# Rotated keys from exchanged half-head tiles, a mask by quarters, and a shorter correlation tail

## The reference

```python
x = x + tanh(g_xattn[0]) * attention_16_heads_of_8(norm(x), ctx, ctx)   # |i - j| > 64 masked
x = x + tanh(g_ffn[0])   * experts_8_top_2(norm(x))
x = x + tanh(g_xattn[1]) * latent_attention(ctx, norm(x))               # 8 heads of 64, rope on the keys of ctx
x = x + tanh(g_ffn[1])   * experts_16_top_2_and_shared(norm(x))
x = x + tanh(g_xattn[2]) * attention_16_heads_of_8(norm(x), ctx)        # with projections
x = x + tanh(g_ffn[2])   * receptance(norm(x))
x = x + tanh(g_xattn[3]) * autocorrelation(norm(x), ctx, ctx)
x = x + tanh(g_ffn[3])   * experts_8_top_2_of_512(norm(x))
```

## Time and profile before

| | us |
|---|---|
| median of 3 runs | 956.03 |
| lowest, highest | 952.27, 965.45 |
| profiled execution | 957.7 |
| its span | 955.9 |
| TensorE busy in the span | 804.1 |
| VectorE, ScalarE, GpSimd busy | 603.4, 510.3, 415.1 |

### The profile page before, as it was taken

One profiled execution on the slowest core, in us unless ns is written; L12 is line 12 of the kernel. 1 busy time (PEld: TensorE's weight loads), 2 busy tenths in 40 slices (PEclk: granted clock), 3 DMA queues, 4 the chain that ended last, 5 costly groups with the idle time before them and its releaser, 6 DMA issues. The chain is left out here.

```text
span 955.9 us, 21238 instructions
## 1 busy us (share of the span) xinstructions
PE 804.1 (84%) x6318; PEld 607.5 (64%) x6318; DVE 603.4 (63%) x1841; ACT 510.3 (53%) x1423; POOL 415.1 (43%) x705
## 2 busy tenths in 40 slices
PE   4999996997579999999978974999988856869992
PEld 1466664796457777777755762666658634639992
DVE  5799985343456777777655435899957745743333
ACT  1466664674046656656643651677764422316663
POOL 2356655001524456655333006566517414743442
PEclk9999998899599999999998985799998977569996
DMA  8999910342000000000002441000000222122214
GB/s 277 377 409 405 314 52 30 84 95 55 17 6 13 10 16 25 18 19 18 13 15 67 111 109 29 18 19 19 13 1 2 62 73 81 46 61 55 69 55 148
DMA packets 69278, 78.96 MB, mean 83 GB/s; under 512 B 12848, under 2 KB 58560, under 8 KB 68912
## 3 DMA queue, kind: packets, MB, share of 16 engines
q1 hardware_dynamic: 60256, 62.74, 20.7%
q0 software_dynamic: 6368, 13.38, 4.8%
q10 hardware_dynamic: 2544, 1.48, 0.6%
HBM read 31.61 MB, written 45.96 MB: 81 GB/s over the span
## 5 line engine op out<-in xcount | busy, mean ns | idle before, releaser
L324 POOL DMA_INDIRECT routed_region<-routed_lines,line_slots x96 | 96.6, 1006 | 27.8 <-issue 22.4
L356 POOL DMA_INDIRECT late_results<-routed_region,line_slots x64 | 63.5, 992 | 80.4 <-DVE work L639 64.2
L1340 PE MATMUL banks<-exps,work 128*128 128x128 f32 x624 | 85.6, 281 | 5.3 <-ACT exps L1414 5.1
L891 PE MATMUL banks<-work,weights_a 128*128 128x128 f32 x512 | 77.4, 296 | 14.0 <-ACT work L1121 8.2
L259 POOL TENSOR_TENSOR small<-small,half_and_eps 128x1 f32<-128x1 f32 x144 | 83.8, 582 | 11.3
L773 ACT ACTIVATE probs_keymajor<-banks 128x512 f32<-128x512 f32 x128 | 69.9, 595 | 34.0 <-PE banks L569 34.0
L1340 PEld LDWEIGHTS banks<-exps,work 128*128 128x128 f32 x624 | 77.9, 196 | 7.6 <-ACT exps L1414 7.3
L644 DVE TENSOR_REDUCE small<-banks 128x8 f32<-128x1024 f32 x64 | 77.6, 1212 | 7.9 <-PE banks L543 7.7
L543 PE MATMUL banks<-work 32*128 32x512 f32 x256 | 81.7, 718 | 0.0
L653 DVE TENSOR_TENSOR exps<-banks,small 128x1024 f32<-128x1024 f32 x64 | 77.7, 1214 | 3.8 <-PE banks L569 3.4
L891 PEld LDWEIGHTS banks<-work,weights_a 128*128 128x128 f32 x512 | 65.2, 199 | 23.1 <-ACT work L1121 10.2
(11 more groups left out here) (283 smaller groups left out, 1932.8 us busy)
## 6 DMA issues: line engine op xcount, KB each, us to landing
routed_region<-mid SPq DMA_DIRECT2D x52, 528.0 KB, 5.4
exps<-routed_region SPq DMA_DIRECT2D x125, 66.0 KB, 2.0
routed_region<-work SPq DMA_DIRECT2D x86, 64.0 KB, 1.8
weights_f<-in_weights_f SPq DMA_DIRECT2D x1, 4096.0 KB, 17.4
weights_f<-in_weights_f SPq DMA_DIRECT2D x3, 1024.0 KB, 11.1
shifted_rows<-work SPq DMA_DIRECT2D x16, 128.0 KB, 1.7
work<-expert_results SPq DMA_DIRECT2D x8, 256.0 KB, 4.5
routed_region<-routed_lines,line_slots POOLq DMA_INDIRECT x96, 2.4
```

The source lines that it names most:

```text
L324: nc.gpsimd.indirect_dma_start(k.regions[layer % 2], bass.IndirectOffsetOnAxis(k.slots[:, b, j:j + 1], 0), k.line[:, b % LINES, j, :], Non ...
L356: nc.gpsimd.indirect_dma_start(k.late[:, b % 2, j, :], None, k.regions[layer], bass.IndirectOffsetOnAxis(k.slots[:, b, j:j + 1], 0)).then_ ...
L891: last = nc.tensor.matmul(bank[:, MA, p * T:(p + 1) * T], k.w[weight][:, p * 128:(p + 1) * 128], kvT[:, sl, part * T:(part + 1) * T], star ...
L1340: last = nc.tensor.matmul(bank[:, 2 + m % 4, i * T:(i + 1) * T], tile.weights[:, m % COPIES, i * 128:(i + 1) * 128], tile.gotT[:, m % 2, : ...
```

## The change

The rotated keys get no matmul of their own: the weights of keys and queries are copied once, by ScalarE, so that the first halves of all heads stand in tiles 0 and 1 and the second halves in tiles 2 and 3 (`by_half`; the copied keys' weights take the place of `wkrot1`, the queries' that of `wk1`). The product by sin reads the same bank as that by cos, and GpSimd takes the other half's tile of it, subtracting in the first half and adding in the second, for which the sign in the table of sines is undone. Scores then multiply 32 rows and accumulate the two halves. The mask comes after the scores, and only into the two quarters of each bank where it is not zero. The correlation's tail works on the negated values, folds steps together, and divides last; the mirrored values are made in its waits; the circulants are loaded from its end by two queues; the bias is added per element. The orders of all engines in the first and the latent attention are new.

The lists of semaphores and tiles, the bank numbers of the tail, and the removed parts of functions whose new form is shown are left out:

```diff
+            for first in (0, L1D):
+                sin = c["sin"][first:first + L1D // 2, :]
+                nc.vector.tensor_scalar(sin, sin, -1.0, None, ALU.mult).then_inc(s.ready, 1)
...
-                    if masked:
-                        for g in range(first, first + 2):
-                            nc.tensor.matmul(bank[:, g, :], k.maskb[:, 0:128], k.maskb[:, 128:], start=True, stop=False)
                     for g in range(first, first + 2):
                         rows_ = slice(32 * g, 32 * g + 32)
                         last = nc.tensor.matmul(bank[:, g, :], qT[rows_, sl, :],
                                                 kx[rows_, sl, :, :].rearrange("p j t -> p (j t)"),
-                                                start=not masked, stop=True)
+                                                start=True, stop=not masked)
+                    if masked:
+                        for g in range(first, first + 2):
+                            for near, far in ((0, WINDOW), (WINDOW, 0)):
+                                rows_ = slice(near, near + WINDOW)
+                                last = nc.tensor.matmul(split(bank[rows_, g, :], T)[:, :, far:far + WINDOW],
+                                                        k.maskb[rows_, near:near + WINDOW],
+                                                        split(k.maskb[rows_, 128:], T)[:, :, far:far + WINDOW],
+                                                        start=False, stop=True)
                     last.then_inc(s.scores, 1)
...
-                 [(scores(0), 1), (in_T, 0), (logits, 6), (probs(0), 3), (output_transpose, 4), (probs(2), 3),
-                  (ranks, 6), (out_T, 4), (scores(2), 1), (out, 4), (pv, 3), (next_T, 5)])
+                 [(pv, 3), (in_T, 0), (next_T, 5), (scores(2), 1), (ranks, 6), (logits, 5), (probs(0), 2),
+                  (output_transpose, 3), (probs(2), 2), (out_T, 3), (scores(0), 0), (out, 3)])
...
-                 [(norm_out, 8), (stats_in, 0), (add, 7), (maximum(1), 4), (stats_out, 7), (shift(1), 4),
-                  (chosen, 8), (maximum(0), 3), (divide, 6), (norm_in, 1), (shift(0), 3), (placed, 8)])
+                 [(shift(1), 5), (stats_in, 0), (chosen, 9), (norm_out, 8), (add, 7), (maximum(0), 4),
+                  (stats_out, 7), (shift(0), 4), (placed, 9), (maximum(1), 4), (divide, 6), (norm_in, 1)])
...
-                 [(dev_out, 7), (counted, 8), (spread_values, 5), (bias, 4), (spread_keys, 1), (sent, 8),
-                  (dev_in, 0)])
+                 [(dev_in, 0), (dev_out, 6), (bias, 2), (sent, 8), (spread_values, 2), (counted, 7),
+                  (spread_keys, 1)])
...
-                 [(out_T, 5), (exps, 3), (next_T, 6), (outputs, 4), (queries, 0), (logits, 6), (probs_out, 3)])
+                 [(logits, 6), (probs_out, 3), (out_T, 4), (exps, 2), (next_T, 5), (outputs, 3), (queries, 0)])
...
+    by_half = {"wk1": k.w["wkrot1"], "wq1": k.w["wk1"]}
...
-            def scores(half):
+            def scores(group):
                 def stage(b, sl):
                     wait(pe, s.q, b + 1)
                     wait(pe, s.k_ctx, b + 1)
                     wait(pe, s.k_lat, b + 1)
-                    wait(pe, s.exp, L1H * b - (L1H // 2 if half == 0 else 0))
-                    for p in range(2 * half, 2 * half + 2):
-                        for par in range(2):
-                            rows_ = slice(64 * par, 64 * par + 64)
-                            last = nc.tensor.matmul(bank[:, 2 * half + par, (p % 2) * 256:(p % 2) * 256 + 256],
-                                                    qT[rows_, sl, p, :], kT[rows_, sl, p, :], start=True, stop=True)
+                    wait(pe, s.exp, L1H * b)
+                    for dims in range(2):
+                        for r in range(4):
+                            rows_ = slice(32 * r, 32 * r + 32)
+                            last = nc.tensor.matmul(bank[:, r, group * 256:group * 256 + 256],
+                                                    qT[rows_, sl, 2 * dims + group, :], kT[rows_, sl, 2 * dims + group, :],
+                                                    start=dims == 0, stop=dims == 1)
                     last.then_inc(s.scores, 1)
...
-            k_rot = project("wkrot1", 0, s.k2, lambda b: wait(pe, s.t1, b + 1))
-            k_lat = project("wk1", 1, s.k3, lambda b: wait(pe, s.t2, b + 1))
+            k_lat = project("wk1", 1, s.k3, lambda b: (wait(pe, s.t1, b + 1), wait(pe, s.t2, b + 1)))
...
-                            n = 4 * (p // 2) + 2 * par + p % 2
+                            n = 2 * (h % 4) + h // 4
...
-            walk(pe, [(out, 4), (shared_gate(0), 4), (k_ctx, 1), (probs(0), 3), (k_rot, 1), (probs(2), 3), (next_T, 5), (k_lat, 1),
-                      (logits, 5), (query, 1), (pv, 3), (values(0), 1), (ranks, 6), (scores(0), 1), (values(1), 1),
-                      (scores(1), 1), (in_T, 0), (shared_up, 4), (shared_gate(1), 5)])
+            pe.wait_ge(s.halved, 4)
+            walk(pe, [(scores(0), 1), (in_T, 0), (scores(1), 1), (k_ctx, 0), (out, 3), (shared_gate(0), 3),
+                      (probs(0), 2), (k_lat, 0), (probs(2), 2), (next_T, 4), (query, 0), (pv, 2), (values(0), 0),
+                      (logits, 4), (values(1), 0), (ranks, 5), (shared_up, 3), (shared_gate(1), 4)])
...
-                wait(dve, s.k2, b + 1)
+                wait(dve, s.k1, b + 1)
+                wait(dve, s.k_ctx, b)
...
-            walk(dve, [(rope_cos, 2), (norm_out, 6), (chosen, 7), (rope_sin, 2), (maximum, 3), (logits, 6),
-                       (norm_in, 1), (stats_in, 0), (values, 2), (stats_out, 5), (placed, 7), (norm_latent, 1),
-                       (normalise, 3), (add, 4)])
+            walk(dve, [(normalise, 4), (rope_sin, 2), (rope_cos, 2), (norm_out, 6), (add, 5), (maximum, 3),
+                       (stats_out, 5), (norm_in, 1), (chosen, 7), (norm_latent, 1), (values, 2), (logits, 6),
+                       (stats_in, 0), (placed, 7)])
...
-                nc.gpsimd.tensor_tensor(kT[:, sl, :, 0:T], split(t1, T), split(t2, T), ALU.add).then_inc(s.k_ctx, 1)
+                now, turned = split(t1, T), split(t2, T)
+                nc.gpsimd.tensor_tensor(kT[:, sl, 0:2, 0:T], now[:, 0:2, :], turned[:, 2:4, :], ALU.subtract)
+                nc.gpsimd.tensor_tensor(kT[:, sl, 2:4, 0:T], now[:, 2:4, :], turned[:, 0:2, :], ALU.add).then_inc(s.k_ctx, 1)
...
-            walk(pool, [(counted, 9), (dev_out, 7), (rope_add, 3), (sent, 9), (dev_latent, 2), (keep, 7),
-                        (fetched, 0), (dev_in, 1)])
+            walk(pool, [(dev_out, 7), (dev_in, 2), (rope_add, 3), (keep, 9), (dev_latent, 2), (counted, 9),
+                        (fetched, 0), (sent, 9)])
...
-            walk(act, [(k_lat, 1), (query, 1), (exps, 2), (values, 1), (outputs, 3), (in_T, 0), (probs(0), 2),
-                       (probs(2), 2), (next_T, 4)])
+            act.wait_ge(ld.weights[2], 16)
+            for n, name in enumerate(("wk1", "wq1")):
+                if n:
+                    act.wait_ge(s.halved, 2)
+                halves = k.w[name].rearrange("p (h x d) -> p x h d", x=2, d=L1D // 2)
+                for x in range(2):
+                    nc.scalar.activation(split(by_half[name][:, 256 * x:256 * x + 256], L1D // 2), halves[:, x],
+                                         ACT.Copy).then_inc(s.halved, 1)
+            walk(act, [(in_T, 0), (outputs, 3), (probs(0), 2), (k_lat, 0), (probs(2), 2), (next_T, 4), (query, 0),
+                       (exps, 1), (values, 0)])
...
+    def load_circulants(queue, parts):
+        for part in parts:
+            from_, to = PARTS[part:part + 2]
+            queue.dma_start(circ[:, from_:to, :], bass.AP(scratch_c.tensor, from_ * 2 * T,
+                                                          [[1, T], [2 * T, to - from_], [1, T]])).then_inc(ld.circ[part], 16)
...
+            def mirror(q):
+                for b in range(4 * q, 4 * q + 4):
+                    last = nc.tensor.matmul(bank[:, q, (b % 4) * T:(b % 4 + 1) * T], c["mirror"], at(vtok, b),
+                                            start=True, stop=True)
+                last.then_inc(s.vm, 1)
+
+            def mirrors(b, sl):
+                if b == B - 2:
+                    pe.wait_ge(s.qk_out, B)
+                    pe.wait_ge(s.v, B)
+                if b >= B - 2:
+                    mirror(b - (B - 2))
+
+            walk(pe, [(products, 3), (in_T, 0), (project, 1), (means, 10), (mirrors, 6)])
...
+            nc.tensor.matmul(bank[0:B, 5, 256:256 + T], eqT, c["earlier"], start=True, stop=True).then_inc(s.rank, 1)
+            mirror(2)
+            pe.wait_ge(s.ex, 1)
+            nc.tensor.transpose(bank[:, 6, 128:128 + B], ex, c["ident"][0:B, 0:B]).then_inc(s.exT, 1)
+            pe.wait_ge(s.exT_out, 1)
+            nc.tensor.matmul(bank[0:B, 6, 256:256 + T], exT, c["mirror"], start=True, stop=True).then_inc(s.cr, 1)
+            mirror(3)
...
```

(62 more changed lines are left out.)

## The result

| | before | changed |
|---|---|---|
| median, us (4 runs each) | 958.09 | 916.38 |
| lowest to highest | 952.27 to 965.45 | 913.33 to 920.29 |
| profiled execution, its span | 957.7, 955.9 | 913.43, 911.6 |

The ratio is 0.9545, with a 95% interval of 0.9502 to 0.9589: 41.7 us by the medians, 44.3 by the two profiled executions. The changed kernel's profile was taken three more times in the groups of experiments: ratios 0.9562, 0.9561 and 0.9573.

The account below looks back on a forecast made before the run. TensorE and its order bound both attentions; a VectorE, GpSimd and DMA chain bound the tail, indirect sends the roll block. Gains 6.4 + 16 + 5.2 = 27.6 us, from 957.7 to 930.1 profiled, written as a 929 median; range 919 to 944.

Parts of the forecast that it names:

- New cost 0.22 + 0.19 = 0.41, as before: First attention's mask: four quarters stream 0.22 plus 0.19 shape change and drain per call, so 0 us gained.
- the period under the new order: First attention: period falls from 8.00 to TensorE's busy 7.80; 12 periods by 0.20 give 2.4 us.
- The term of 4 us for the end: First attention's end: one of five steps between last mask and last rank goes, 5.2 us each, taken as 4.
- k_rot's 1.00: Latent attention: the rotated keys' four matmuls, 1.00 us of TensorE per element, go.
- -0.17 (values(1), and logits and ranks closer packed): Latent attention's period: 0.17 us less per element from these TensorE groups, within 14.37 to 13.45.
- the printed 0.45: Latent attention: the query projection's wait for the copy out of its PSUM bank, 0.45 us per element, becomes covered.
- The new orders only move the waits: Rival on both attentions: half the latent gain (8) and the 4 of the drain lost, 941 us; chance 0.17.
- The chain: Correlation tail, small steps on VectorE and ScalarE up to the write: fewer steps and no mean copy save 1.7 us.
- 5.2 earlier: Correlation tail and roll block: first aggregate at 789.7 instead of 794.89 us; bounds 3 and 7.
- Four row tiles in each other's way: Rival on the latent scores: call takes 1.5 us, +14 us, kernel 943; chance 0.08.
- two by two: Rival: 32-row score tiles run in pairs (call 1.93 us) and mask quarters singly, kernel 964 us; chance 0.06.
- More than forecast: Rival: full period and earlier full clock in first attention, 19 us in latent attention, kernel 919; chance 0.04.

Follow-up runs that it names:

- quarters_only: Kernel before with only the mask's quarters placed behind the scores, old orders kept; ratio to before 0.9894 (0.9841 to 0.9947).
- The table of four: Old or new latent arithmetic with old or new orders; periods: both old 14.38 us, only orders new 14.29, only arithmetic new 15.50, both new 13.09.
- warm: Changed kernel plus idle bf16 products at the start of the latent attention (44) and next attention (38); ratio to before 0.9642, not used because ScalarE stalled.

## Why the prediction was right on the mechanism and too low on the gain

- **First attention: 12.0 for 6.4.** The failed step is the sentence "New cost 0.22 + 0.19 = 0.41, as before". The cost before was not 0.41: the row has 0.52, and the paragraph had just taken 0.09 out of it as drain. By its own numbers the mask should have been priced at -0.11 per call; measured is -0.10, with the quarters side by side as assumed and the shape change paid as assumed. The rule of the Trainium skill's page "TensorEngine Tiling (Array Packing)", section "Key Properties", that a change of tiling mode drains the engine, agrees with the run: in quarters_only the start of the scores moves from 0.17 to 0.26 behind the transpose. The second mis-sized term is the period under the new order: the order took 0.37 from it, the wait of 0.20 as forecast and 0.17 of TensorE's own time, which I held fixed. The last nine intervals between input transposes take 67.4 us instead of 72.0, where I had 2.4 for twelve. The term of 4 us for the end was right, but not as I put it: from the last input transposes to the last rank it is 7.1 us less, and 3.0 of them come back at the start. The first six intervals take 42.3 us instead of 39.3 where the clock rises at like times, because the first probabilities now come into them, at 30 us instead of 34.4, while TensorE is still at 1.2 GHz. The rest is luck, the moment at which the clock first rose to 2.4 GHz. In four profiles of the same changed kernel the last rank is at 154.3 to 157.2; the latest has that moment at 38.9 us, near the 39.2 of before, the one of the result at 32.7. At like clocks the stage gained 9.1, and 2.9 of its 12.0 came with the clock.
- **Latent attention: 22.9 for 16.** The shape of the argument held: k_rot's 1.00 gone, the wait for the query gone, a wait of 0.66 (forecast 0.7) in its place, a scores call of 1.07 (1.06), the exponentials in time. The mis-sized term is "-0.17 (values(1), and logits and ranks closer packed)". Between the two timelines `out` shortened by 0.17, `probs(0)` and `k_lat` by 0.07 each, `query` and `values(1)` by 0.10 each and `logits` by 0.11, against 0.13 more around the scores: -0.49. A part of it was in the trace of before, in its view of the weight loads:

```profile
381.07 0.97 PEld L891 LDWEIGHTS banks<-work,weights_a 128*128 128x128 f32 x8 [0.19 <-ACT work L1104]
...
383.01 0.97 PEld L891 LDWEIGHTS banks<-work,weights_a 128*128 128x128 f32 x8
```

The first row is k_ctx's. It starts 0.05 us after ScalarE's copy of its operand ends (381.02), and `out`, ahead of it, is followed after 1.06 us where it is followed after 0.89 in the changed kernel: 0.17 of the 0.49 was this wait, and it is gone because the copy now runs beside `scores(1)`. k_rot's first load starts together with its first matmul, at 383.01, and VectorE's product that releases it ends at 382.96; the wait is too short to be printed. In the changed kernel k_lat's load stands 0.11 ahead (332.76 and 332.87). So the bank's chain was tight at k_rot too, and its groups were longer for it. I read the printed 0.45 as the only wait of the chain. That such waits explain the rest of the 0.49 is argued, not shown; the 0.1 that k_ctx still pays in the changed kernel is the shape. The thirteen intervals gave 16.8 for 12, the first two 4.1 for 3.1, the drain 2.0 for 0.9.
- **What I did not see in the latent attention** is that the new arithmetic needs the new orders. "The new orders only move the waits" was priced at half the gain lost. The table of four shows that the old orders lose all of it and 12.6 us more.
- **Tail: 4.5 for 5.2.** The chain gave 1.48 for 1.7, the write to the aggregate 3.06 for 3.5, the mirror groups cost nothing, and the sends set the roll block's pace as said. Between first aggregate and first send 0.6 was given back: TensorE was at 1.2 GHz there from 739.2, and before for 5.4 of 9.5 us. "5.2 earlier" was written as the sum of edits; bias and early loads are nearly alternatives.
- **Unchanged stages: 6.4 for 0.** From the last latent rank to the first in_T of the next attention it is 70.5 to 71.8 us in the thirteen profiles that have both new arithmetic and new orders in the latent attention (without `warm`), and 72.9 to 75.5 in the six others. From that rank to the end of the experts 0 to 7.9 us were at 1.2 GHz in the thirteen and 9.7 to 13.8 in the six. So about 2.6 us (71.1 against 73.7 in the mean) come with the change, and the rest is scatter. That they come through the clock is argued from this sorting; why the clock stays up behind the new latent attention was not tested. The 108.2 to 112.8 us of the next attention in all these profiles do not sort by kernel: its 2.3 us are chance. I gave these stages no width.
- **The rivals.** Four row tiles in each other's way, and two by two, fell with the call of 1.07. "More than forecast", 919, had 0.04 and was nearest. Each of its terms was an end that I had named, 10 and 19 for the attentions; both were passed. The range should have been wider below by the clock's scatter and by TensorE time that a new order itself can save.

## To carry to other kernels

A saving of arithmetic and the order that goes with it are one edit: price them on the new layout's dependencies (here eight exponentials for a call instead of four), since either alone can be worth nothing or less. When a new cost is said to be "as before", put the row of before beside it once more, whole, with the drain in it. Around a chain through one buffer look for groups whose weight load starts with the matmul and not ahead of it: they wait although no wait is printed, or they stand behind a change of tile shape. And a lag taken from the end of a stage is partly paid at its start: count both ends.

## What the runs showed of the hardware that was not expected

- Four row tiles of 32 rows, 128 outputs and 256 columns run together at no loss: 1.07 us for two times four of them, 1.06 for two times two of 64 rows. Four bf16 quarters of 64 x 64 with 256 columns take 0.33 to 0.34 with the shape change behind the scores.
- The moment of the first rise to 2.4 GHz lay between 31.8 and 45.9 us with the same first attention; where it was 45.9 the stage's last rank was at 160.9, where it was 32.7 at 154.3.
- ScalarE stood idle for 2.6 to 3.2 us, five to seven times in one stage, with no releaser in the trace, in three profiles of one group and in no other. The cause is open.
- In the four profiles of that same group the first attention's period was 7.8 instead of 7.5 us, and the 32 sends of the roll block took 45.6 to 46.5 us instead of 44.0.
